# Local-attention scores as 64-row products per head, and value products on 64-key halves with 32-row edges

## The chip, the cores and the metric

The kernel runs on one NeuronCore of a Trainium2 chip. The time is the device time of one execution in microseconds (us). The runs of the kernel before have a median of 3595.3 us (three runs, 3594.93 to 3595.39).

## The reference, cut to what matters

The input is 16 sequences of 256 tokens with 128 features, all float32. First comes one causal attention layer with 16 heads of 8 features. Its output, layer-normalised, enters a stack of six layers, and each layer does, for every sequence:

```python
qkv = x @ Wqkv                                   # 128 -> 3 * 1024
q, k, v = 16 heads of 64
q, k = l2norm, times a scale, rotary turn
# local attention: windows of 32 queries, each sees its own 32 keys and the 32 before them
sim  = einsum('bhwie,bhwje->bhwij', bq, bk2) * 8     # 32 queries x 64 keys
attn = softmax(where(mask, -big, sim))               # j from i to i + 32 only
out  = einsum('bhwij,bhwje->bhwie', attn, bv2)       # 64 keys x 64 features
x = x + out @ Wo
# half of the features shifted by one token, layer norm, gated feed-forward
x = x + (a * gelu(gate)) @ W2 + b2
```

The change concerns the two einsum lines of the local attention.

## The kernel before, in words

The unit of work in the stack is one sequence in one layer, so there are 96 units, in order of layers. A sequence is two tiles of 128 tokens (t = 0 and 1). The first layer (causal attention) comes before and is not touched.

**The pipeline.** Each engine has its own queue, written out by hand in a function `step`, and works strictly in that order; semaphores tie the queues together. Step n works on three units at once: the "head" of unit n (projections of q, k, v and their norms), the "mid" of unit n-1 (turning q and k, scores, softmax, band) and the "ffn" of unit n-2 (values of tile 1, output projection, feed-forward). 94 of the 98 steps hold all three parts.

**PSUM.** `PJ` is the two banks of the projections, `TR[0]` and `TR[1]` are one bank each for transposes and the hidden layer, `EXO` and `EXY` half a bank each for the outputs. `SC` is two banks, `SC[:, 0]` and `SC[:, 1]`. They hold the scores of 8 heads each, and, in turn with them, the products with the values.

**Scores** (`scores(n, t, g)`, line 1389). g is a half of the heads and a bank. Before it, ScalarE writes the additive mask into the bank (`put_mask`, line 665) and the product is added to it. Two heads share 128 rows of `qT` (64 rows each). The keys are stored in `kbd` as a block-diagonal pair: head 0's keys in rows 0 to 63 with zeros under them, head 1's in rows 64 to 127 with zeros above. One product of 128 rows, 32 queries and 2 x 64 columns so gives two heads of one window. A block has 16 products, 4 windows in 4 column groups of the array, each writing 32 partitions. `k_evac` (lines 647 and 648) copies the turned keys into `kbd` in two instructions of 64 partitions each.

**Softmax.** VectorE takes the row maximum (`row_max`, line 901) and subtracts it (`less_max`, line 906), for each half g; ScalarE takes the exponential of a whole tile (`exps`, line 603); VectorE sums (913, 916), GpSimd normalises (462), and VectorE turns the tile in 32x32 blocks into `PTr[t]` (`turn`, line 923).

**Band and values.** SyncE's queue copies `PTr[t]` with DMAs into `BD`, which for each of four windows is a zero matrix of 128 keys with a band of 64 keys filled (`band`, lines 309 and 311, 7 DMAs a tile). For tile 1 the queries of the first window also need the last 32 keys of tile 0: `BB` (4 DMAs) holds their weights and `Vx` (4 DMAs, `edge_values`) the values. `values(n, t, g)` (lines 1344 and 1349) multiplies 128 keys by 4 windows of 32 queries for each of the 8 heads of half g, and for tile 1 adds the edge with two more products. ScalarE copies the result to `oT` (`o_evac`, line 672), and `output` (line 1356) multiplies by Wo.

**Order on TensorE in a full step** (m = n-1, f = n-2): turn_x(n), turn_k(m,0,0), output(f,0), turn_k(m,0,1), project_q(n,0), turn_q(m,0,0), values(f,1,0), turn_q(m,0,1), values(f,1,1), scores(m,0,0), output(f,1), scores(m,0,1), turn_q(m,1,0), turn_q(m,1,1), turn_k(m,1,0), project_v(n,0), scores(m,1,0), turn_k(m,1,1), project_k(n,0), scores(m,1,1), turn_xn(f), project_v(n,1), hidden(f,0), hidden(f,1), project_q(n,1), values(m,0,0), hidden(f,2), values(m,0,1), project_k(n,1), feed_out(f).

**Order on ScalarE**, the part around the change: q_evac(m,0,0), o_evac(f,1,0), put_mask(m,0,0), o_evac(f,1,1), q_evac(m,0,1), put_mask(m,0,1), squares, put_mask(m,1,0), q_evac(m,1,0), q_evac(m,1,1), exps(m,0), k_evac(m,1,0), put_mask(m,1,1), v_evac(n,0), rsqrt_guess(f) (lines 512 and 514), k_evac(m,1,1), keep_raw(n,0,k), xn_evac(f), squares, exps(m,1), v_evac(n,1), the gelus, ...

**Order on VectorE**, the same part: row_max and less_max(m,0,0), residual1(f) (line 1001, waits for output(f,1)), row_max and less_max(m,0,1), sum_q, soft_sum(m,0), x2_moments(f) (waits for the DMAs of the shift that start from residual1), row_max(m,1,0), ln_roots(f) (1026 to 1030), turn(m,0), layer_norm(f) (line 1038, whose result turn_xn(f) waits for), less_max(m,1,0), row_max and less_max(m,1,1), sum_k, soft_sum(m,1), cosines, gated(f,0), turn(m,1), ...

The trace counts passes: every float32 product runs as two passes with a weight load each, so a block of 16 products appears as x32. A transpose is one pass.

Of the kernel before, what the change touches and what calls it, by code (L numbers as in the profile page):

```python
# [10 lines left out]
ACT = mybir.ActivationFunctionType  # L11
# [38 lines left out]
def build(nc, x_in, wq_t, wk_t, wv_t, wo_t, wqkv, q_scale, k_scale, wo2, ln_g, ln_b, w1, b1, w2, b2,  # L50
          c_ident, c_winmask, c_causal, c_headmask, c_rot, out):
    with ExitStack() as ctx:
# [3 lines left out]
        def sem(name):  # L56
# [85 lines left out]
        names = ("d_x d_x2 d_wa d_wap d_rot d_c d_wq d_wk d_wv d_qks d_wo d_ln d_ff d_out i_const i_zero i_pad i_dve i_pool i_sp i_guess i_bits d_id d_wav d_hm "  # L142
# [5 lines left out]
                 "s_tab s_ct s_nq s_nk d_bd0 d_bd1 d_vx")  # L148
        S = {n: sem(n) for n in names.split()}
        (d_x, d_x2, d_wa, d_wap, d_rot, d_c, d_wq, d_wk, d_wv, d_qks, d_wo, d_ln, d_ff, d_out, i_const, i_zero, i_pad, i_dve, i_pool, i_sp, i_guess, i_bits, d_id, d_wav, d_hm,  # L150
# [5 lines left out]
         s_tab, s_ct, s_nq, s_nk, d_bd0, d_bd1, d_vx) = [S[n] for n in names.split()]  # L156
# [13 lines left out]
        N_BAND = (2 * NWIN - 1, 2 * NWIN - 1 + 4)  # L170
        N_VX = 4
# [68 lines left out]

        def turn_of_k(n, t):
            return 4 * n + (4 if t else 1)
# [13 lines left out]
        def _(sp):  # L256
# [46 lines left out]
            def band(n, t):  # L303

                need_apart(sp, i_sp, s_T, 2 * n + t + 1)
                need_apart(sp, i_sp, s_o, 4 * n + 2 * t - 2)
                for w in range(NWIN):
                    rows = slice(32 * w, 32 * w + 32)
                    sp.dma_start(BD[rows, t, w, :, :], PTr[t][rows, 1, :, :]).then_inc(d_bd[t], 16)
                    if w:  # L310
                        sp.dma_start(BD[32 * w - 32:32 * w, t, w, :, :], PTr[t][rows, 0, :, :]).then_inc(d_bd[t], 16)
                if t:
                    edge = PTr[t][0:WIN, 0, :, :].rearrange("p (g c k) i -> p g c (k i)", g=2, c=4)
                    for c in range(4):
                        sp.dma_start(BB[32 * c:32 * c + 32, :, c, :, :].rearrange("p g k i -> p g (k i)"),
                                     edge[:, :, c, :]).then_inc(d_bd[t], 16)

            def edge_values(n, par):

                need_apart(sp, i_sp, s_ve, 2 * n + 1)  # L320
                need_apart(sp, i_sp, s_o, 4 * n - 4)
                last = V[par][P - WIN:P, 0, :].rearrange("p (g c n) -> p g c n", g=2, c=4)
                for c in range(4):
                    sp.dma_start(Vx[32 * c:32 * c + 32, par, :, :], last[:, :, c, :]).then_inc(d_vx, 16)
# [10 lines left out]
            def step(n, u, par, head, mid, ffn, layer, more=False):  # L335
# [28 lines left out]
        def _(pool):  # L364
# [9 lines left out]
            pool.memset(BB[:, :, :, :, :], 0.0).then_inc(i_zero, 1)  # L374
            pool.wait_ge(d_hm, 16)
            pool.wait_ge(i_zero, 5)
# [13 lines left out]
            def a_step(n, par, head, mid, tail):  # L390
                if head:
                    spread_k(n, par)
                    if isinstance(n, int) and n == 0:
                        pool.memset(kbd[:, :, :, :], 0.0).then_inc(i_zero, 1)
# [106 lines left out]
        def _(act):  # L501
# [88 lines left out]
            act.wait_ge(i_zero, 7)  # L590
# [43 lines left out]
            def v_evac(n, t, par):  # L634
                T = 2 * n + t
                need(act, s_pv, T + 1)
                need(act, s_o, 4 * n - 4)
                act.activation(V[par][:, t, :], PJ[:, :], ACT.Copy).then_inc(s_ve, 1)  # L638

            def k_evac(n, t, g):  # L640
# [3 lines left out]
                need(act, s_sc, 4 * n - 1 + g)  # L644
                c = slice(4 * g, 4 * g + 4)
                at = slice(WIN + P * t, WIN + P * t + P)
                act.activation(kbd[0:DH, c, 0, at], tr[0:DH], ACT.Copy)
                act.activation(kbd[DH:P, c, 1, at], tr[DH:P], ACT.Copy).then_inc(s_te[g], 1)  # L648

            def q_evac(n, t, g):  # L650
                T = 2 * n + t
                need(act, s_tr[g], turn_of_q(n, t))
                need(act, s_sc, 2 * T - 1 + g)
# [14 lines left out]
            def o_evac(n, t, g):  # L668
                need(act, s_o, 4 * n + 2 * t + g + 1)
# [879 lines left out]
```

## Time and profile before

| | |
|---|---|
| median of the runs | 3595.3 us |
| span of the profiled execution | 3598.4 us |
| TensorE busy | 3482.8 us, 97% |
| VectorE busy | 3160.0 us, 88% |
| ScalarE busy | 3061.0 us, 85% |
| GpSimd busy | 2352.0 us, 65% |
| score passes (L1389) | 12288, busy 415.6 us |
| value passes (L1344, L1349) | 6144 and 768, busy 421.5 and 74.7 us |

The profile holds one execution; its span from the first to the last instruction is all that the page gives of its time, and it is 3.1 us over the median of the runs. Busy time counts overlapping instructions once. A TensorE row in a timeline ends with the modelled end of its last pass, about 0.1 to 0.2 us after the engine could take the next one; where one row starts before the one above has ended, the difference of the starts is what the first really took.

### The profile page before, as it was taken

How to read it: one execution, taken by the hardware profiler on the slowest of the kernel's cores; microseconds unless marked ns; L12 is line 12 of the kernel's file. 1: busy time of each engine (PE TensorE's matmuls, PEld its weight loads, DVE VectorE, ACT ScalarE, POOL GpSimd, SP SyncE). 2: the span in 40 equal slices, each digit the busy share in tenths (PEclk: the TensorE clock that was granted, in tenths of full speed). 3: DMA queues.
4: the chain of work that ended last, by engine and by line, in shares of the span. 5: the costliest groups of instructions: out<-in, count | busy, mean ns of one | idle time of the engine just before them, and what ended most of it. 6: DMA issues, size and time to landing. Idle time of an engine off the chain costs nothing.

```text
span 3598.4 us, 95666 instructions
## 1 busy us (share of the span) xinstructions
PE 3482.8 (97%) x33868; PEld 2390.4 (66%) x33868; DVE 3160.0 (88%) x5848; ACT 3061.0 (85%) x5121; POOL 2352.0 (65%) x1607
## 2 busy tenths in 40 slices
PE   8999899999999999999999999999999999999998
PEld 6777466666666666666666666666666666666666
DVE  6998889888988988888888898888889888888986
ACT  5766688888888888888888888888888888888886
POOL 2001677777777777777777677777777777777774
PEclk9999999999999999999999999999999999999999
DMA  2000011112211112211112111112111112211112
GB/s 63 0 0 0 21 34 39 38 33 54 52 34 34 39 36 52 50 40 33 34 40 53 46 39 38 32 36 58 47 33 39 38 33 55 52 33 34 39 37 54
DMA packets 182965, 136.67 MB, mean 38 GB/s; under 512 B 97612, under 2 KB 135632, under 8 KB 182800
## 3 DMA queue, kind: packets, MB, share of 16 engines
q1 hardware_dynamic: 180019, 125.00, 14.8%
q10 hardware_dynamic: 2781, 9.51, 0.9%
q8 instruction: 98, 1.61, 0.2%
q14 instruction: 67, 0.55, 0.1%
HBM read 19.04 MB, written 2.10 MB: 6 GB/s over the span
## 4 chain that ended last, share of the span: by engine, by line
PE 62%; ACT 19%; issue 10%; DVE 5%; SPq 1%; POOL 1%; DMA 1%; ACTq 0%; DVEq 0%; POOLq 0%
PE ps L1302 12%; PE ps L1389 10%; PE ps L1356 10%; PE ps L1344 7%; PE ps L1379 4%; PE ps L1370 4%; PE ps L1160 3%; ACT L750 3%; ACT area L603 2%; DVE area L987 2%; ACT G L609 2%; ACT L609 2%; ACT area L618 2%; ACT area L625 2%; PE ps L1295 2%
## 5 line engine op out<-in xcount | busy, mean ns | idle before, releaser
L1302 PE MATMUL ps<-Wqkv,xsT 128*128 128x512 f32 x2304 | 1112.5, 605 | 8.7 <-ACT area L638 3.8
L449 POOL TENSOR_TENSOR area<-area,tab 128x512 f32<-128x512 f32 x768 | 970.0, 1273 | 146.7 <-ACT area L618 146.1
L1302 PEld LDWEIGHTS ps<-Wqkv,xsT 128*128 128x128 f32 x2304 | 391.2, 189 | 351.4 <-issue 295.0
L462 POOL TENSOR_TENSOR area<-area,lsum 128x1024 f32<-128x1024 f32 x192 | 365.5, 1904 | 383.2 <-DVE lsum L916 383.2
L456 POOL TENSOR_TENSOR AQb<-AQb,area 128x1024 f32<-128x1024 f32 x192 | 455.2, 2371 | 15.1
L456 POOL TENSOR_TENSOR area<-area 128x1024 f32<-128x1024 f32 x192 | 455.0, 2370 | 9.0 <-DVE area L976 1.5
L618 ACT ACTIVATE area<-ps 128x1024 f32<-128x1024 f32 x384 | 393.6, 1025 | 66.2 <-PE ps L1302 55.1
L1389 PEld LDWEIGHTS ps<-kbd,area 128*32 128x32 f32 x12288 | 313.2, 109 | 196.1 <-issue 113.4
L1344 PE MATMUL ps<-BD,area 128*64 128x128 f32 x6144 | 421.5, 279 | 17.7 <-issue 11.3
L1344 PEld LDWEIGHTS ps<-BD,area 128*64 128x64 f32 x6144 | 329.4, 137 | 158.8 <-issue 100.2
L1389 PE MATMUL ps<-kbd,area 128*32 128x128 f32 x12288 | 415.6, 276 | 17.0 <-ACT kbd L648 5.7
L625 ACT ACTIVATE area<-area 128x1024 f32<-128x1024 f32 x384 | 405.1, 1055 | 3.2
L1356 PE MATMUL ps<-Wo,area 128*128 128x128 f32 x3072 | 385.2, 279 | 1.2 <-ACT area L672 0.7
L1356 PEld LDWEIGHTS ps<-Wo,area 128*128 128x128 f32 x3072 | 357.6, 192 | 20.7 <-issue 19.6
L654 ACT ACTIVATE area<-ps 128x512 f32<-128x512 f32 x384 | 217.9, 593 | 132.6 <-PE ps L1379 132.6
L901 DVE TENSOR_REDUCE mx<-ps 128x8 f32<-128x512 f32 x384 | 263.2, 686 | 49.7 <-PE ps L1389 49.7
L923 DVE STREAM_TRANSPOSE area<-area 128x1024 f32<-128x1024 f32 x192 | 239.2, 1246 | 61.7 <-POOL area L462 61.2
L1295 PE MATMUL ps<-xnT,W 128*128 128x256 f32 (+1 forms) x1152 | 288.3, 386 | 1.8 <-ACT xnT L684 1.5
L672 ACT ACTIVATE area<-ps 128x512 f32<-128x512 f32 x384 | 227.0, 591 | 71.0 <-PE ps L1349 66.8
L906 DVE TENSOR_TENSOR area<-ps,mx 128x512 f32<-128x512 f32 x384 | 264.8, 690 | 9.9
L1295 PEld LDWEIGHTS ps<-xnT,W 128*128 128x128 f32 (+1 forms) x1152 | 197.8, 178 | 91.3 <-issue 63.6
L941 DVE TENSOR_REDUCE ss<-area 128x16 f32<-128x1024 f32 x192 | 233.6, 1216 | 22.4 <-ACT area L625 21.2
(136 smaller groups left out, 6630.6 us busy)
## 6 DMA issues: line engine op xcount, KB each, us to landing
BD<-area SPq DMA_DIRECT2D x1344, 64.0 KB, 2.0
Vx<-area SPq DMA_DIRECT2D x384, 32.0 KB, 1.9
Wqkv<-ffn_Wqkv ACTq DMA_DIRECT2D x18, 512.0 KB, 4.0
BB<-area SPq DMA_DIRECT2D x384, 16.0 KB, 1.8
x2s<-x2s SPq DMA_DIRECT2D x96, 56.0 KB, 2.0
Wo<-ffn_Wo SPq DMA_DIRECT2D x6, 512.0 KB, 4.3
W<-ffn_W SPq DMA_DIRECT2D x6, 341.0 KB
x2s<-x2s SPq DMA_DIRECT2D x96, 0.2 KB, 1.7
```

What stands on the lines that cost most here:

```text
L449: pool.tensor_tensor(b4[:, :, here], q4[:, :, there], s4[:, :, here], ALU.mult).then_inc((s_bq, s_bk)[j], 1)
L456: pool.tensor_tensor(AQ[t][:, col], AQ[t][:, col], BQ[:, col], ALU.add).then_inc(s_rot, 1)
L462: pool.tensor_tensor(p3, p3, lsum[:, 1, :].unsqueeze(2).broadcast_to([P, HEADS, 2 * WIN]), ALU.mult).then_inc(s_pn, 1)
L618: act.activation(QH[:, j * INNER:(j + 1) * INNER], PJ[:, :], ACT.Copy).then_inc((s_hq, s_hk)[j], 1)
L625: act.activation(SQ[:, col], QH[:, col], ACT.Square).then_inc((s_sqq, s_sqk)[j], 1)
L901: dve.tensor_reduce(mx[:, 8 * g:8 * g + 8], s3[:, g, :, :], AX.X, ALU.max).then_inc(s_mx, 1)
L906: dve.tensor_tensor(Pr[:, t, 512 * g:512 * g + 512].rearrange("p (h k) -> p h k", k=2 * WIN), s3[:, g, :, :], mx[:, 8 * g:8 * g + 8].unsqu ...
L1295: last = mm(TR[c % 2][0:m, half * SEQ:(half + 1) * SEQ], W1[:, half * FF + f0:half * FF + f0 + m], xnT[:, :], start=True, stop=True)
L1302: last = mm(PJ[:, b * 512:(b + 1) * 512], xsT[:, par, t * P:(t + 1) * P], Wqkv[:, w0:w0 + 512], start=True, stop=True)
L1344: last = mm(slot[DH * k:DH * k + DH, c * P:(c + 1) * P], V[par][:, t, h * DH:(h + 1) * DH], BD[:, t, :, h, :], start=(c == 0), stop=False, ...
L1356: last = mm(EXO[:, t * P:(t + 1) * P], oT[:, t, c, :], Wo[:, c, :], start=(c == 0), stop=(c == PAIRS - 1))
L1389: last = mm(SC[32 * w:32 * w + 32, g, (c % 4) * P:(c % 4 + 1) * P], qT[:, c, 32 * w:32 * w + 32], kbd[:, c, :, k0:k0 + 2 * WIN], start=Fal ...
```

## The change

Scores become one product per head and window: the 64 rows of the head's q and of its keys, in the 64-row half of the array where they lie. The keys lose their zeros (`kT`), and are copied in one instruction. The even head of a pair writes bank 0 and the odd head bank 1, so one call now fills both banks, and there is one `scores` call a tile instead of two. Where the heads lie in a score tile changes with it (`place`).

Values: the band of a tile is now two halves of 64 keys with two windows of queries each (`BD`), and the windows that reach 32 keys into the half (or the tile) before get these as 32-row products (`BE`). The first half of the keys writes bank 0, the second bank 1; one `values` call a tile replaces two. `BB`, `Vx` and their DMAs go, and tile 1 has 8 band DMAs instead of 11.

The waits of these two calls on TensorE go through `need_apart`, which waits and then raises a semaphore that nobody waits for. Nothing is changed in the order of the other engines' queues: `row_max`, `less_max`, `put_mask`, `o_evac` stay at their places and work bank by bank.

```diff
-        kbd = sb("kbd", [P, PAIRS, 2, WIN + SEQ])
-        BD = sb("BD", [P, TILES, NWIN, HEADS, WIN])
-        BB = sb("BB", [P, 2, 4, 2, WIN])
-        Vx = sb("Vx", [P, 2, 2, P])
+        kT = sb("kT", [P, PAIRS, WIN + SEQ])
+        BD = sb("BD", [P, TILES, 2, HEADS, WIN])
+        BE = sb("BE", [P, TILES, HEADS, WIN])
...
+        def place(h):
+            return (h % 2) * PAIRS + h // 2
...
             def band(n, t):
                 need_apart(sp, i_sp, s_T, 2 * n + t + 1)
-                need_apart(sp, i_sp, s_o, 4 * n + 2 * t - 2)
+                need_apart(sp, i_sp, s_o, 2 * n + t - 1)
+                rows = [slice(32 * w, 32 * w + 32) for w in range(NWIN)]
                 for w in range(NWIN):
...
+                    sp.dma_start(BD[rows[w], t, w % 2, :, :], PTr[t][rows[w], 1, :, :]).then_inc(d_bd[t], 16)
+                    if w % 2:
+                        sp.dma_start(BD[rows[w - 1], t, 1, :, :], PTr[t][rows[w], 0, :, :]).then_inc(d_bd[t], 16)
+                    elif w or t:
+                        sp.dma_start(BE[rows[w - 1], t, :, :], PTr[t][rows[w], 0, :, :]).then_inc(d_bd[t], 16)
...
                 if mid:
                     band(n - 1, 0)
-                    edge_values(n - 1, 1 - par)
                     band(n - 1, 1)
...
             def k_evac(n, t, g):
...
-                need(act, s_sc, 4 * n - 1 + g)
-                c = slice(4 * g, 4 * g + 4)
+                need(act, s_sc, 2 * n)
                 at = slice(WIN + P * t, WIN + P * t + P)
-                act.activation(kbd[0:DH, c, 0, at], tr[0:DH], ACT.Copy)
-                act.activation(kbd[DH:P, c, 1, at], tr[DH:P], ACT.Copy).then_inc(s_te[g], 1)
+                act.activation(kT[:, 4 * g:4 * g + 4, at], tr, ACT.Copy).then_inc(s_te[g], 1)
...
             def o_evac(n, t, g):
-                need(act, s_o, 4 * n + 2 * t + g + 1)
+                need(act, s_o, 2 * n + t + 1)
...
             def row_max(n, t, g):
                 T = 2 * n + t
-                need(dve, s_sc, 2 * T + g + 1)
+                need(dve, s_sc, T + 1)
...
+            def values(n, t, par):
+
+                need_apart(pe, i_pe, s_ve, 2 * n + t + 1)
+                need_apart(pe, i_pe, d_bd[t], 16 * N_BAND[t] * (n + 1))
+                if t:
+                    need_apart(pe, i_pe, s_oe, 4 * n + 2)
+                else:
+                    need_apart(pe, i_pe, s_sub, 4 * n + 4)
+                for c in range(PAIRS):
+                    for r in range(2):
+                        keys = slice(2 * WIN * r, 2 * WIN * (r + 1))
+                        for k in range(2):
+                            h = 2 * c + k
+                            mm(SC[DH * k:DH * k + DH, r, 2 * WIN * c:2 * WIN * (c + 1)], V[par][keys, t, h * DH:(h + 1) * DH],
+                               BD[keys, t, :, place(h), :], start=(c == 0), stop=False, skip_group_check=True)
+                for c in range(PAIRS):
+                    for k in range(2):
+                        h = 2 * c + k
+                        last = mm(SC[DH * k:DH * k + DH, 1, 2 * WIN * c:2 * WIN * c + WIN], V[par][WIN:2 * WIN, t, h * DH:(h + 1) * DH],
+                                  BE[WIN:2 * WIN, t, place(h), :], start=False, stop=True, skip_group_check=True)
                     if t:
+                        for k in range(2):
+                            h = 2 * c + k
+                            last = mm(SC[DH * k:DH * k + DH, 0, 2 * WIN * c:2 * WIN * c + WIN], V[par][P - WIN:P, 0, h * DH:(h + 1) * DH],
+                                      BE[P - WIN:P, t, place(h), :], start=False, stop=True, skip_group_check=True)
                 last.then_inc(s_o, 1)
...
+            def scores(n, t):
+
+                ready = turn_of_k(n, 1) if t else turn_of_q(n, 0)
+                need_apart(pe, i_pe, s_mk, 4 * n + 2 * t + 2)
+                need_apart(pe, i_pe, s_te[0], ready)
+                need_apart(pe, i_pe, s_te[1], ready)
+                for c in range(PAIRS):
                     for w in range(NWIN):
                         k0 = P * t + WIN * w
+                        for k in range(2):
+                            half = slice(DH * k, DH * k + DH)
+                            last = mm(SC[32 * w:32 * w + 32, k, 2 * WIN * c:2 * WIN * (c + 1)],
+                                      qT[half, c, 32 * w:32 * w + 32], kT[half, c, k0:k0 + 2 * WIN],
+                                      start=False, stop=True, skip_group_check=True)
                 last.then_inc(s_sc, 1)
...
                 if ffn:
-                    values(n - 2, 1, 0, par)
+                    values(n - 2, 1, par)
                 if mid:
                     turn_q(n - 1, 0, 1)
                 if ffn:
-                    values(n - 2, 1, 1, par)
-                if mid:
-                    scores(n - 1, 0, 0)
-                if ffn:
                     output(n - 2, 1)
                 if mid:
-                    scores(n - 1, 0, 1)
+                    scores(n - 1, 0)
                     turn_q(n - 1, 1, 0)
...
                 if mid:
-                    scores(n - 1, 1, 0)
                     turn_k(n - 1, 1, 1)
...
                 if mid:
-                    scores(n - 1, 1, 1)
+                    scores(n - 1, 1)
...
-                if mid:
-                    values(n - 1, 0, 0, 1 - par)
                 if ffn:
                     hidden(n - 2, 2)
                 if mid:
-                    values(n - 1, 0, 1, 1 - par)
+                    values(n - 1, 0, 1 - par)
```

## Rows read from the trace of the kernel before

**Rows 1.** The page: span, and busy time of each engine.
```profile
span 3598.4 us, 95666 instructions
PE 3482.8 (97%) x33868; PEld 2390.4 (66%) x33868; DVE 3160.0 (88%) x5848; ACT 3061.0 (85%) x5121; POOL 2352.0 (65%) x1607
```

**Rows 2.** Timeline of TensorE: start, duration, line, shapes, count [idle before, releaser].
```profile
1688.89 1.09 PE L1344 MATMUL ps<-BD,area 128*64 128x128 f32 x16
...
1690.13 1.08 PE L1389 MATMUL ps<-kbd,area 128*32 128x128 f32 x32
1691.14 2.05 PE L1356 MATMUL ps<-Wo,area 128*128 128x128 f32 x16
1693.13 1.08 PE L1389 MATMUL ps<-kbd,area 128*32 128x128 f32 x32
1694.14 1.09 PE L1379 MATMUL ps<-ident,AQb 128*128 128x128 f32 x8
1695.58 0.65 PE L1370 MATMUL ps<-ident,AQb 128*128 128x128 f32 x4 [0.35 <-ACT area L654]
1696.07 1.88 PE L1302 MATMUL ps<-Wqkv,xsT 128*128 128x512 f32 x4
1698.08 1.08 PE L1389 MATMUL ps<-kbd,area 128*32 128x128 f32 x32
```

**Rows 3.** Timeline of TensorE one unit later, the same place.
```profile
1728.62 0.66 PE L1370 MATMUL ps<-ident,AQb 128*128 128x128 f32 x4 [0.33 <-ACT area L654]
```

**Rows 4.** Timeline of TensorE in two windows of 0.05 and 0.03 us.
```profile
1690.13 0.32 PE L1389 MATMUL ps<-kbd,area 128*32 128x128 f32 x4
...
200.83 0.38 PE L1149 MATMUL ps<-area,AqT 32*128 32x128 f32 x2
```

**Rows 5.** Timeline of ScalarE around the scores.
```profile
1690.25 0.60 ACT L672 ACTIVATE area<-ps 128x512 f32<-128x512 f32 x1 [0.60 <-PE ps L1349]
...
1692.83 0.60 ACT L665 ACTIVATE ps<-wmask_f 128x512 f32<-128x512 f32 x1
1694.93 1.09 ACT L654 ACTIVATE area<-ps 128x512 f32<-128x512 f32 x2 [1.49 <-PE ps L1379]
...
1696.85 0.58 ACT L647 ACTIVATE kbd<-ps 64x512 f32<-64x512 f32 x1
...
1698.54 1.03 ACT L638 ACTIVATE area<-ps 128x1024 f32<-128x1024 f32 x1
```

**Rows 6.** Timeline of VectorE around the scores.
```profile
1692.11 0.69 DVE L906 TENSOR_TENSOR area<-ps,mx 128x512 f32<-128x512 f32 x1
1693.36 0.42 DVE L1001 TENSOR_TENSOR x2s<-ps,xres 128x256 f32<-128x256 f32 x1 [0.56 <-PE ps L1356]
1694.27 0.69 DVE L901 TENSOR_REDUCE mx<-ps 128x8 f32<-128x512 f32 x1 [0.49 <-PE ps L1389]
...
1699.52 0.69 DVE L901 TENSOR_REDUCE mx<-ps 128x8 f32<-128x512 f32 x1
```

**Rows 7.** Timeline of all engines: layer_norm and the transpose behind it.
```profile
1701.86 0.57 DVE L1038 SCALAR_TENSOR_TENSOR xn<-x2s,mv,ps 128x128 f32<-128x128 f32 x2
...
1702.55 0.44 PE L1285 MATMUL ps<-ident,xn 128*128 128x128 f32 x2
```

**Rows 8.** Timeline of TensorE: rows that follow a long idle time.
```profile
397.34 2.65 PE L1389 MATMUL ps<-kbd,area 128*32 128x128 f32 x64 [1.85 <-ACT ps L665]
...
1942.45 1.09 PE L1344 MATMUL ps<-BD,area 128*64 128x128 f32 x16 [1.56 <-issue]
...
3566.46 1.97 PE L1344 MATMUL ps<-BD,area 128*64 128x128 f32 x16 [2.34 <-issue]
```

**Rows 9.** Windows after them: busy time by engine, granted clock, DMA share, GB/s.
```profile
398.70:402.00 3.30, 3.18 (x36) 2.40 (x26) 2.85 (x5) 0.73 (x2) 1.67 (x2) 0.50 0.03 7
...
1942.40:1946.00 3.60, 3.55 (x37) 2.57 (x38) 2.92 (x4) 2.02 (x3) 3.60 (x5) 1.00 0.52 174
...
3566.40:3569.40 3.00, 2.94 (x19) 2.32 (x20) 1.61 (x2) 0.00 (x0) 1.05 (x1) 0.50 0.21 44
```

More of the change, by code:

```diff
@@ L155, in build @@
          s_o, s_oe, s_ve, s_wo, s_r1, d_sh, s_lnc, s_lnr, s_lnn, s_ln, s_xn, s_xne, s_h, s_gl, s_g, s_y, s_xc,
-         s_tab, s_ct, s_nq, s_nk, d_bd0, d_bd1, d_vx) = [S[n] for n in names.split()]
+         s_tab, s_ct, s_nq, s_nk, d_bd0, d_bd1) = [S[n] for n in names.split()]
         PJ = ps[:, 0:2, :].rearrange("p a b -> p (a b)")
@@ L169, in build @@
         N_FF = 8
-        N_BAND = (2 * NWIN - 1, 2 * NWIN - 1 + 4)
-        N_VX = 4
+        N_BAND = (2 * NWIN - 1, 2 * NWIN)
         d_bd = (d_bd0, d_bd1)
@@ L589, in _ @@
             attention_steps(act, a_step)
-            act.wait_ge(i_zero, 7)
+            act.wait_ge(i_zero, 6)
             def x_evac(n, par):
@@ L668, in o_evac @@
             def o_evac(n, t, g):
-                need(act, s_o, 4 * n + 2 * t + g + 1)
+                need(act, s_o, 2 * n + t + 1)
                 if t == 0 and g == 0:
                     need(act, s_wo, n)
-                act.activation(oT[:, t, 4 * g:4 * g + 4, :], SC[:, g, :].rearrange("p (c n) -> p c n", c=4),
+                half = slice(2 * WIN * g, 2 * WIN * (g + 1))
+                act.activation(oT[:, t, :, half], SC[:, g, :].rearrange("p (c n) -> p c n", c=PAIRS),
                                ACT.Copy).then_inc(s_oe, 1)
@@ L1326, in project_v @@
                 projected(n, t, par, 2, s_pv)
-            def values(n, t, g, par):
-                T = 2 * n + t
-                if g == 0:
-                    need(pe, s_ve, T + 1)
-                    if t:
-                        need(pe, d_vx, 16 * N_VX * (n + 1))
-                    need(pe, d_bd[t], 16 * N_BAND[t] * (n + 1))
-                if t:
-                    need(pe, s_oe, 4 * n + g + 1)
-                else:
-                    need(pe, s_sub, 4 * n + 3 + g)
-                slot = SC[:, g, :]
-                for c in range(4):
-                    for k in range(2):
-                        h = 2 * (4 * g + c) + k
-                        last = mm(slot[DH * k:DH * k + DH, c * P:(c + 1) * P], V[par][:, t, h * DH:(h + 1) * DH],
-                                  BD[:, t, :, h, :], start=(c == 0), stop=False, skip_group_check=True)
-                if t:
-                    for k in range(2):
-                        half = slice(DH * k, DH * k + DH)
-                        last = mm(slot[half, :].rearrange("p (c n) -> p c n", c=4)[:, :, 0:WIN], Vx[:, par, g, half],
-                                  BB[:, g, :, k, :], start=False, stop=True, skip_group_check=True)
@@ L1380, in turn_q @@
                 last.then_inc(s_tr[g], 1)
-            def scores(n, t, g):
-                need(pe, s_mk, 4 * n + 2 * t + g + 1)
-                need(pe, s_te[g], turn_of_k(n, 1) if t else turn_of_q(n, 0))
-                for c in range(4 * g, 4 * g + 4):
+            def scores(n, t):
[4 more added lines that the diff above has]
+                for c in range(PAIRS):
                     for w in range(NWIN):
                         k0 = P * t + WIN * w
-                        last = mm(SC[32 * w:32 * w + 32, g, (c % 4) * P:(c % 4 + 1) * P],
-                                  qT[:, c, 32 * w:32 * w + 32], kbd[:, c, :, k0:k0 + 2 * WIN],
-                                  start=False, stop=True, skip_group_check=True)
+                        for k in range(2):
[3 more added lines that the diff above has]
+                                      start=False, stop=True, skip_group_check=True)
                 last.then_inc(s_sc, 1)
```

30 lines of the change are left out of this document (7 added, 23 removed).

## The prediction, as written before the changed kernel was run

> **What bounds the kernel now.** I read the page first. The reader is to see that TensorE is busy 97% of the span, VectorE 88% and ScalarE 85% [rows 1]. So TensorE's queue sets the pace, but two engines stand close behind it, and their queues were laid out around TensorE's order. Next the timeline of TensorE over one unit. The same transposes, behind the same short wait, start at 1695.58 and at 1728.62: a unit takes 33.04 us [rows 2, 3]. In it TensorE waits 0.35 us for ScalarE ahead of those transposes, and 0.29 ahead of the third score block, which starts at 1698.08 where the projection of 1696.07 (1.88 less an overlap of 0.16, so 1.72) ends at 1697.79 [rows 2]. With about 0.3 for small ones (my estimate) the waits are 0.95 a unit. There are 94 units in the full pattern, so 1 us a unit is 94 us, 2.6% of the time.
>
> **What TensorE gains: scores.** A block of 32 passes takes 1.01 us (1690.13 to 1691.14, and 1693.13 to 1694.14), and there are four a unit: 4.04 us [rows 2]. The four column groups work side by side: in a window of 0.05 us four passes have started [rows 4]. So 32 passes are eight rounds of 128 columns, about 0.11 each, and 0.14 remains for getting in from the whole array. The new block has 128 passes of 64 columns, eight tiles to a round, so 16 rounds. If the two 64-row halves run side by side, a round is 0.055 and the block 0.88 + 0.14, say 1.03. For the halves the trace has no row; the nearest is the causal layer, where two passes in different 32-row groups start within 0.03 us and write different banks [rows 4], as the two heads do here. I take 1.03 (bounds 0.9, and 1.9 if the halves take turns). Two blocks are 2.06: a gain of 1.98.
>
> **Values.** A 16-pass block takes 1.09 less 0.07 of overlap, 1.02, and with the edge of tile 1 1.24 (1688.89 to 1690.13) [rows 2]: 2 x 1.02 + 2 x 1.24 = 4.52 a unit. The new call has 64 passes of 64 columns on four tiles (16 rounds of 0.055), then an edge part of 32 passes on two tiles or 64 on four (16 rounds). The edge has only 32 columns but loads 64 weight columns, so I give it 0.055 a round too. With 0.14 for getting in and 0.14 for the change from 64 to 32 rows: 0.88 + 0.88 + 0.28 = 2.04, twice 4.08, a gain of 0.44. Bounds for one call: 1.5 if the edge goes at the speed of its columns, 2.9 and 3.9 (tiles 0 and 1) if row groups take turns.
>
> **Fewer changes of shape.** Output takes 1.99 (1691.14 to 1693.13) where 16 passes at 0.11 are 1.76 [rows 2]: of the 0.23, some 0.16 is the way back to the whole array. Eight blocks become four, which gives 0.65. TensorE gains 1.98 + 0.44 + 0.65 = 3.1 us a unit, 29.0 of work instead of 32.1.
>
> **What it loses: the two banks no longer take turns.** Today, while one half of the heads is with VectorE or ScalarE, TensorE works on the other. Now a call needs both banks and frees both, while the queues of the other engines stay as they are. I walk these queues with the row durations. A block's result reaches the next engine 0.13 us after it (1694.14 to 1694.27) [rows 2, 6]; between engines I add 0.08.
>
> (a) output(f,1) needs both o_evac. Behind the values ScalarE does o_evac, put_mask, o_evac (0.60, 0.60, 0.60 [rows 5], in sequence with overlap 1.75), so it can start 0.13 + 1.75 + 0.08 = 1.96 after the values. In that time TensorE has turn_q, 0.59 behind a block. Wait 1.4. Today the first o_evac and the mask run under the second block.
>
> (b) turn_k(m,1,0) needs q_evac(m,1,0), which on ScalarE stands behind put_mask(m,1,0), which needs the first less_max. From the end of scores: 0.13 + row_max 0.71 (0.69 and a gap of 0.02) + less_max 0.69 + 0.08 + mask 0.60 + q_evac 0.55 + 0.08 = 2.84 [rows 5, 6]. TensorE has two calls of turn_q, 1.04. Wait 1.8, in place of 0.35. Today output(f,1) and the second block cover this chain.
>
> (c) project_k needs v_evac, behind exps. VectorE after scores: 0.13 + 0.71 + 0.69, residual1 0.42 (rounded up to 0.45), row_max 0.71, less_max 0.65 (with overlap), 0.08: 3.4. ScalarE then does exps 0.97 (1.03 for this size, less overlap, as in v_evac's row), k_evac 0.55 (one instruction at a 128x512 copy's time, in place of two of 0.58), put_mask 0.58, v_evac 0.95 [rows 5]: 6.5. TensorE is there at 2.84 + turn_k 0.50 + project_v 1.74 + turn_k 0.44 = 5.5. Wait 1.0, and 0.2 more ahead of scores(m,1), for the last k_evac.
>
> (d) turn_xn needs layer_norm. On VectorE this stands behind row_max(m,1,0), the three small ln_roots and turn(m,0). Today row_max starts at 1699.52, under the transposes and project_k, and the xn rows from 1701.86 to 1702.43 are just in time for the transpose at 1702.55 [rows 6, 7]. In the new order scores(m,1) is one block directly ahead of turn_xn, and row_max can't start before its end. Start of row_max to end of xn is 2.91 without a gap, so the wait is 0.13 + 2.91 = 3.0. This is the largest, and it hangs on no unknown of the array.
>
> (e) Behind turn_xn ScalarE's and VectorE's queues are late as well (they have xn_evac, squares, sum_k, soft_sum(m,1), cosines and gated(f,0) to do before hidden(f,2) can start), while TensorE comes through its four projections and hidden blocks at its old speed. I allow 0.9 for what it waits at project_q(n,1) and hidden(f,2), an estimate with bounds 0 and 2.
>
> Sum of waits: 1.4 + 1.8 + 1.0 + 0.2 + 3.0 + 0.9 = 8.3, less today's 0.95. A unit grows by 8.3 - 0.95 - 3.1 = 4.2 us, to 37.3. Over 94 units that is 395 us.
>
> **What costs nothing.** ScalarE's four k_evac save 2.3 us a unit, but the walk has them in it. Of the DMAs 7 of 22 in a unit go; the values of tile 0 wait for their 7 either way, and the layer's turn(m,0) to values(m,0) grows longer, so they stay hidden. The added semaphore increments are off the chain as long as their semaphores are early; they stop TensorE's sequencer from running ahead, up to 0.1 at a block that was late (between 0 and 0.4 a unit; I take 0). The causal layer is untouched.
>
> **The clock.** Three idle stretches of TensorE, the first and last of them 1.85 and 2.34 us, were each followed by a stretch at half clock (0.50, 1.2 GHz); one of 1.56 was not, and the clock stayed at 1.00 (2.4 GHz) [rows 8, 9]. Values passes took 1.97 for 16 there, against 1.09 [rows 2, 8]. Wait (d) is 3.0 and comes in every unit, so I expect half clock behind it in most: about 3.3 us in which 1.7 of work takes 3.4. Of the extra 1.7, the 0.9 of (e) is absorbed, and the rest delays ScalarE's gelus: 1.0 a unit, in 0.8 of the units 75 us.
>
> **The sum.** The span is 3598.4 and the median of runs 3595.3; the 3 us between them don't matter to a growth, which I add to the median: 3595 + 395 + 75 = 4065 us.
>
> **A page that speaks against the change.** In a window of 0.05 us four passes on different column groups start, and 32 take 1.01 us, 31.6 ns each [rows 2, 4]. The Trainium skill, "TensorEngine Tiling (Array Packing)", section "Instruction Overhead", says that each matmul has some 60 cycles of overhead on this chip and that a dimension already small should not be tiled. If that held per pass and not per tile, 25 ns at 2.4 GHz (an estimate from that page), scores would take 3.2 and values 2.4 and 3.2, and the result would be near 4540; the rows speak for the shared reading.
>
> **Rivals.**
> 1. No half clock, or seldom: 3595 + 395 = 3990. For it: the waits of 1.56 and less left the clock alone. Chance 0.27.
> 2. The row halves take turns, or passes are bound by their number. With 1.9 for scores and 2.9 and 3.9 for values the calls add 2 x 0.87 + 0.86 + 1.86 = 4.5: 395 + 420 gives about 4410. At today's 31.6 ns for every pass they would be 4.04, 3.03 and 4.04, 9.0 more a unit: some 4840. Against it: rows 4. Chance 0.13.
> 3. Half clock behind (b) as well, 1.8 long and near the 1.85 that was enough once: another 1.2 a unit, 4180. Chance 0.10.
> 4. Faster. If the waits were covered as they are today, the unit would fall from 33.04 to the busy time of VectorE, 88.5% of it or 29.3, and about 1 of its waits: 30.3, in all 3340. It decides at (d): row_max(m,1,0) would have to come before TensorE wants turn_xn. Faster blocks alone don't do it: at the low bounds, 0.9 and 1.5, a unit still takes 37.3 - 0.3 - 1.1 = 35.9, so the sign turns only where (d) and one more wait are covered. Chance 0.04.
> The likeliest (0.46) is 4065.
>
> **How the numbers follow.** What can be told from no change is about 0.2%. Only rival 4 is faster, and a part of 0.02 I leave for waits that just balance the gain; slower has the rest, 0.94. The range goes from below rival 1 with a short edge part (a unit 1 us less: 3900) to above rival 3 (4260); left out are rival 2, rival 4 and the ends.
>
> **What would show it.** Score passes: x128 blocks of about 1.0 us, twice a unit. Ahead of turn_xn about 3 us of idle TensorE, released by VectorE's layer_norm; ahead of output(f,1) 1.4 by o_evac, of turn_k(m,1,0) 1.8 by q_evac, of project_k(n,0) 1.0 by v_evac. TensorE's share of busy time falls from 97% to about 80%. The clock: dips behind turn_xn, mean well under 1. The forecast is wrong if the wait at turn_xn is under 2 us, or if the score blocks take over 1.5 us.

## The result, and the profile after

Before 3595.4 us (median of five runs, 3594.9 to 3596.6), after 4342.9 us (five, 4341.4 to 4367.4): 1.209 times as long, 95% interval 1.207 to 1.212. The direction was forecast. The size was not: the growth is 748 us where 470 were forecast, and 4343 lies above the top of the range, 4260. The profiled execution is the slowest of the five, 4367.4 us, some 25 over the median. Of all runs of this document one, of the last kernel below, took 5050.6 us at a granted clock of 0.635 and is left out.

The page of the profile after, at the same places as [rows 1], with the queue of the transfers that bring instructions:

```profile
span 4365.6 us, 148729 instructions
PE 3597.4 (82%) x60748; PEld 2539.6 (58%) x60748; DVE 3172.5 (73%) x5848; ACT 2841.7 (65%) x4737; POOL 2341.1 (54%) x1606
q8 instruction: 521, 8.54, 0.8%
```

All engines fell to 54 to 82%: nothing is full, so TensorE waits. Its waits (engine, line waited for, us in total, times, longest):

```profile
PE ps L1272 <- DVE xn L1025: 280.5, 96, 3.3
PE ps L1359 <- ACT area L640: 152.2, 96, 1.7
PE ps L1345 <- ACT area L659: 122.2, 97, 1.3
PE ps L1289 <- ACT area L626: 72.6, 98, 3.9
PE ps L1382 <- issue: 50.0, 27, 2.4
PE ps L1266 <- issue: 33.7, 30, 1.7
```

The first four are the forecast ones, (d), (b), (a) and (c), about once in each of the 96 units. The last two were not forecast, and no other engine releases them; all waits named "issue" add to 100 us, before to 12.

To see the order of the work alone, take a unit in which the clock stayed up. The timeline of TensorE from one turn_x to the next, which is what [rows 2] show of before (start, duration, line, shapes, count, idle before):

```profile
2745.22 0.43 PE L1266 MATMUL ps<-ident,xst 128*128 128x128 f32 x2 [1.22 <-issue]
...
2750.40 1.16 PE L1328 MATMUL ps<-BD,area 64*64 64x64 f32 x64
...
2752.55 0.66 PE L1368 MATMUL ps<-ident,area 128*128 128x128 f32 x4
2754.49 2.05 PE L1345 MATMUL ps<-Wo,area 128*128 128x128 f32 x16 [1.28 <-ACT area L659]
2756.47 1.49 PE L1382 MATMUL ps<-kT,area 64*32 64x64 f32 x128
2757.88 1.09 PE L1368 MATMUL ps<-ident,AQb 128*128 128x128 f32 x8
2760.61 0.65 PE L1359 MATMUL ps<-ident,AQb 128*128 128x128 f32 x4 [1.63 <-ACT area L640]
...
2764.12 1.99 PE L1289 MATMUL ps<-Wqkv,xsT 128*128 128x512 f32 x4 [0.70 <-ACT area L626]
...
2770.55 0.44 PE L1272 MATMUL ps<-ident,xn 128*128 128x128 f32 x2 [3.03 <-DVE xn L1025]
...
2777.14 1.09 PE L1282 MATMUL ps<-xnT,W 128*85 128x256 f32 x4 [0.69 <-DVE H L916]
...
2783.47 0.38 PE L1266 MATMUL ps<-ident,xst 128*128 128x128 f32 x2
```

The unit takes 38.25 us (2745.22 to 2783.47), before 33.04. A score block takes 1.41 (2756.47 to 2757.88; forecast 1.03), the value call 2.15 (2750.40 to 2752.55; forecast 2.04). The five waits are 1.28, 1.63, 0.70, 3.03 and 0.69. An idle time in this view starts at the modelled end, some 0.1 after the engine was free; from start to start, as the forecast counts, they are about 1.35, 1.7, 0.9, 3.1 and 0.85, together 7.9 (forecast 8.3).

Few units are like this one: only six of the 93 periods between the turn_x of full units have no stretch at half clock, and the three of them that hold no wait named "issue" take 38.3 us on the mean. The mean of the 93 is 41.2. Windows of another unit show the rest (the columns as in [rows 9]: busy time of TensorE, weight loads, VectorE, ScalarE and GpSimd, then granted clock, DMA share, GB/s):

```profile
2008.00:2011.50 3.50, 2.16 (x88) 1.75 (x79) 1.20 (x2) 1.82 (x4) 1.30 (x1) 1.00 0.02 5
2011.80:2015.20 3.40, 3.33 (x16) 3.28 (x16) 1.20 (x2) 1.97 (x4) 0.00 (x0) 0.55 0.00 0
2015.30:2029.20 13.90, 8.70 (x281) 5.73 (x280) 9.13 (x21) 6.68 (x11) 8.18 (x6) 0.98 0.03 7
2029.80:2033.10 3.30, 3.30 (x5) 1.28 (x5) 2.74 (x8) 2.45 (x3) 0.77 (x1) 0.50 0.40 99
```

Two stretches at half clock (0.50, 1.2 GHz; 1.00 is 2.4) in one unit. The first begins at 2011.47, inside wait (a), and lasts into output(f,1); the second begins at 2028.54, inside wait (d), and covers the work behind turn_xn. The trace has 151 such stretches, 4.3 us long on the mean: 57 begin in output(f,1) or the wait ahead of it, 89 in the wait ahead of turn_xn, in turn_xn or in the projection behind it. The mean clock of this execution is 0.926, so 2 x 0.074 x 4365.6 = 646 us of it ran at half clock; before, 0.998 and about 14.

And the unforecast wait, inside a score block:

```profile
2065.22 1.21 PE L1382 MATMUL ps<-kT,area 64*32 64x64 f32 x101
2068.48 0.44 PE L1382 MATMUL ps<-kT,area 64*32 64x64 f32 x27 [2.05 <-issue]
```

101 passes of the block run, then TensorE stands for 2 us with its operands ready, then the other 27. The only DMA traffic between 2065.5 and 2068.5 is one packet of the instruction queue, on its way from 2066.10 to 2067.21. That queue brought 521 packets of 16 KB; before it were 98, and none of them fell between 1695.6 and 1728.6. The whole trace bears this one case out. Of TensorE's 58 "issue" waits over 0.8 us, 56 end between 1.0 and 1.75 us after the end of a packet of this queue, where a tenth of all moments lie. Of the 8 such waits before the change, none does.

So I split the 748 us into three parts, which the experiments below test: (38.3 - 33.04) x 94 = 494 for the order of the work with its real block times, 161 for the clock (from the fillings below), and the remaining 93, which I put down to instruction fetching.

### The profile page after: what moved, and what is told of

It reads as the page before. It is cut to its first block, busy times and chain, and to the rows that moved or that the text cites. A ratio compares the mean times of both kernels' runs of the same rounds, so it can differ in the third digit from the quotient of the medians.

```text
span 4365.6 us, 148729 instructions
## 1 busy us (share of the span) xinstructions
PE 3597.4 (82%) x60748; PEld 2539.6 (58%) x60748; DVE 3172.5 (73%) x5848; ACT 2841.7 (65%) x4737; POOL 2341.1 (54%) x1606
## 4 chain that ended last, share of the span: by engine, by line
PE 69%; DVE 11%; issue 10%; ACT 9%; DMA 0%; DVEq 0%; SPq 0%; ACTq 0%; POOL 0%; POOLq 0%
PE ps L1289 22%; PE ps L1345 10%; PE ps L1382 7%; PE ps L1282 6%; PE ps L1328 4%; PE ps L1333 4%; DVE mx L888 3%; ACT area L659 3%; PE ps L1392 2%; PE ps L1147 2%; PE ps L1359 2%; ACT area L626 2%; DVE area L893 2%; DVE area L910 2%; PE ps L1139 1%
## 5 line engine op out<-in xcount | busy, mean ns | idle before, releaser
L1289 PE MATMUL ps<-Wqkv,xsT 128*128 128x512 f32 x2304 | 1245.1, 668 | 76.2 <-ACT area L626 72.6
L1345 PE MATMUL ps<-Wo,area 128*128 128x128 f32 x3072 | 457.4, 311 | 122.9 <-ACT area L659 122.2
L1345 PEld LDWEIGHTS ps<-Wo,area 128*128 128x128 f32 x3072 | 423.6, 221 | 148.7 <-ACT area L659 145.2
L651 ACT ACTIVATE ps<-wmask_f 128x512 f32<-128x512 f32 x384 | 230.5, 600 | 385.2 <-DVE area L893 382.2
L1382 PEld LDWEIGHTS ps<-kT,area 64*32 64x32 f32 x24576 | 269.5, 110 | 148.5 <-issue 142.9
L1382 PE MATMUL ps<-kT,area 64*32 64x64 f32 x24576 | 305.2, 235 | 54.7 <-issue 50.0
L963 DVE TENSOR_TENSOR area<-area,ps 128x1024 f32<-128x1024 f32 x192 | 228.7, 1191 | 98.1 <-PE ps L1368 97.3
L659 ACT ACTIVATE area<-ps 128x512 f32<-128x512 f32 x384 | 225.0, 587 | 108.0 <-PE ps L1338 106.6
L1272 PE MATMUL ps<-ident,xn 128*128 128x128 f32 x192 | 58.2, 399 | 280.5 <-DVE xn L1025 280.5
L634 ACT ACTIVATE kT<-ps 128x512 f32<-128x512 f32 x384 | 225.6, 588 | 90.3 <-PE ps L1359 87.9
```

The lines of the kernel that those rows point to most:

```text
L651: act.activation(SC[:, g, :].rearrange("p (h k) -> p h k", k=2 * WIN), wmask_f[:, t, :].unsqueeze(1).broadcast_to([P, HEADS // 2, 2 * WIN] ...
L659: act.activation(oT[:, t, :, half], SC[:, g, :].rearrange("p (c n) -> p c n", c=PAIRS), ACT.Copy).then_inc(s_oe, 1)
L1289: last = mm(PJ[:, b * 512:(b + 1) * 512], xsT[:, par, t * P:(t + 1) * P], Wqkv[:, w0:w0 + 512], start=True, stop=True)
L1345: last = mm(EXO[:, t * P:(t + 1) * P], oT[:, t, c, :], Wo[:, c, :], start=(c == 0), stop=(c == PAIRS - 1))
L1382: last = mm(SC[32 * w:32 * w + 32, k, 2 * WIN * c:2 * WIN * (c + 1)], qT[half, c, 32 * w:32 * w + 32], kT[half, c, k0:k0 + 2 * WIN], start ...
```

## The experiments

The theory: the growth is the waits of the walk, the half clock that they bring, and fetches. Rivals: the passes themselves cost it (too many, or the row halves take turns); the clock costs no more than the 75 us of the forecast; the stalls named "issue" are something other than fetching. Each kernel is the changed one with the edit shown, unless said otherwise.

### layer_norm ahead of the late scores on VectorE

```diff
-                if mid:
-                    row_max(n - 1, 1, 0)
                 if ffn:
...
                     layer_norm(n - 2, mid)
                 if mid:
+                    row_max(n - 1, 1, 0)
                     less_max(n - 1, 1, 0)
```

> The changed kernel with one move in VectorE's queue: ln_roots, turn(m,0) and layer_norm stand ahead of row_max(m,1,0) instead of behind it, so they no longer wait for the single score block. Theory A (the waits from the two banks and the unchanged queues make most of the loss, and long waits bring half clock): the 3.0 us wait at turn_xn goes; walking the queues with the durations of the trace gives 36.0 us a unit against 38.3 without clock losses, 216 us less over 94 units, and about 94 more because the longest wait is one of the two that bring half clock: about 4035 us (3950 to 4150). Theory B (the number of passes on TensorE sets the time): within 1% of 4343.

Measured 4079.4 us, ratio to before 1.133 (1.132 to 1.135): 263 us less than the change, from one line's place in VectorE's queue. The expectation was 4035. The waits of TensorE:

```profile
PE ps L1358 <- ACT area L640: 154.3, 96, 1.7
PE ps L1288 <- ACT area L626: 143.5, 175, 2.9
PE ps L1344 <- ACT area L659: 121.3, 97, 1.3
PE ps L1381 <- issue: 47.7, 27, 2.4
```

The 280.5 at the transposes of xn are gone from the list, and a quarter of them come back at the projections, which now wait twice as much for v_evac (72.6 to 143.5). Some of the gain is clock, 0.968 here. What is left of half clock is at the other place: 57 of its 76 stretches begin at output(f,1) or the wait ahead of it, as many as in the change, though the wait at turn_xn is gone. So the stretch at (a) doesn't come from the one at (d).

### TensorE kept busy in the three long waits

bfloat16 products that nobody reads, 5 ahead of output(f,1), 7 ahead of turn_k(m,1,0), 13 ahead of turn_xn. The last place is shown; at the other two a wait for the bank that they write stands ahead of them.

```diff
+                if head and mid and ffn:
+                    fill(TR[0][:, 0:512], 13)
                 if ffn:
                     turn_xn(n - 2)
```

> The changed kernel with bf16 products that nobody reads, put where TensorE waits: 13 ahead of turn_xn, 5 ahead of output(f,1), 7 behind turn_q(m,1,1), each 512 columns, about 0.21 us. They cover the waits without shortening them. Theory A: TensorE is never long idle, the granted clock stays at 1.00, and the 6.3 us of half clock a unit go; by units of the changed kernel with no half clock (38.2 to 38.6) against the mean of 41.0, less the stalls for instructions that remain, about 2 us a unit: 4150 (4080 to 4230). If half clock costs nothing (hidden by the waits): 4343 or a little more.

Measured 4182.4 us, 1.163 (1.161 to 1.165), mean clock 0.996. The unit keeps its order and its pace:

```profile
2402.62 1.67 PE L1405 MATMUL ps<-causal,ident_h 128*128 128x512 bf16 x7
2404.42 0.66 PE L1359 MATMUL ps<-ident,AQb 128*128 128x128 f32 x4
...
2411.26 2.98 PE L1405 MATMUL ps<-causal,ident_h 128*128 128x512 bf16 x13
2414.65 1.88 PE L1289 MATMUL ps<-Wqkv,xsT 128*128 128x512 f32 x4
```

More work on TensorE, and 161 us less time: the waits cost not only themselves but the clock behind them. The projection behind turn_xn takes 1.88 us here and in the clean unit, and 3.62 in a unit with half clock. Most of the 161 is therefore what half clock cost. Not all of it need be: TensorE's waits named "issue" also fell, from 100 to 74 us, most of it in the score blocks (50.0 to 13.9), so the clock's share is 135 to 161.

The run also separates the third part. 89 of the 93 periods have no half clock at all. The 45 of them without an "issue" wait take 38.3 us, as in the change, and the 44 with one take 39.7. Over the 89 the mean is 39.0, so 0.7 x 94, some 70 us, belongs neither to the order of the work nor to the clock.

### Scores alone, and values alone

The first keeps the 128-key bands and values in two blocks, with the new score call; the second keeps the block-diagonal keys and four score blocks, with the new value calls. Of each edit only a part of TensorE's order is shown.

```diff
@@ scores alone
-                    values(n - 2, 1, par)
+                    values(n - 2, 1, 0, par)
                 if mid:
                     turn_q(n - 1, 0, 1)
                 if ffn:
+                    values(n - 2, 1, 1, par)
                     output(n - 2, 1)
...
@@ values alone
+                if mid:
+                    scores(n - 1, 0, 0)
                 if ffn:
                     output(n - 2, 1)
                 if mid:
-                    scores(n - 1, 0)
+                    scores(n - 1, 0, 1)
...
```

> Only the scores are changed (64-row products per head, one block a tile, one k_evac instruction); the products with the values are those of before, on 128 keys, in two halves. Theory A: the walk gives 37.5 us a unit against 32.9 for before: +430 us, plus half clock as in the changed kernel, 100 to 180: about 4170 (4050 to 4260). Theory C (instruction code that no longer fits and is fetched again costs about 0.9 us a unit): if this smaller body fits, instruction packets stay near 98 and no stalls of 1.7 to 2.4 us stand inside score blocks. Theory B, passes: 128 more a unit of the 280, so about 340 us: 3940.

> Only the products with the values are changed (64-key halves, 32-row edges, one call a tile); the scores are those of before. Theory A: values(f,1) frees both banks at once, so scores(m,0,0) waits about 0.9 us for its mask and hidden(f,2) 0.7; the walk gives 34.2 us a unit against 32.9, +123 us, no wait over 1 us, so no half clock: 3720 (3660 to 3800). Theory B, passes: 152 more a unit of the 280: +405 us, 4000. Theory C: if the code fits, no instruction packets above 98.

Scores alone: 4240.0 us, 1.178 (1.176 to 1.180), clock 0.951. Values alone: 3773.4, 1.049 (1.047 to 1.051), clock 0.997. So 645 and 178 us by themselves, and 748 together; the two don't simply add. The longest waits of TensorE, scores alone and then values alone:

```profile
PE ps L1286 <- DVE xn L1039: 280.9, 96, 3.3
PE ps L1371 <- ACT area L655: 158.6, 96, 1.7
PE ps L1303 <- ACT area L641: 77.0, 98, 3.9
PE ps L1357 <- ACT area L673: 67.8, 97, 0.9
PE ps L1394 <- issue: 54.6, 32, 2.2
```

```profile
PE ps L1380 <- ACT ps L653: 79.7, 96, 1.9
PE ps L1284 <- DVE H L918: 69.4, 96, 2.2
PE ps L1268 <- issue: 39.5, 30, 1.7
PE ps L1361 <- ACT area L642: 33.4, 96, 1.2
```

Waits (b), (c) and (d) come whole with the joined score call, as the walk has them. (a) falls to 0.7 a unit, for the first of two value calls gives ScalarE an early start; and of the 84 stretches of half clock only 5 are left at output(f,1), 65 stand at turn_xn, its wait and the projection behind it. Values alone wait 0.8 a unit at a place of their own: the first score block has to wait for the mask, which stands between the two o_evac. The shortest units of it take 34.1 us, 2.0 of that in such waits. Instruction packets are 405 and 427: either half of the change is enough to bring fetches into the loops. (I had thought that each might stay near 98.)

### The kernel before, with a loop body twice as long

```diff
-                with eng.Fori(0, SEQS // 2 - 2) as k:
-                    for odd in range(2):
-                        step(eng.snap(base + 2 * k + (2 + odd)), 2 * k + (2 + odd), odd, True, True, True, layer)
+                with eng.Fori(0, (SEQS // 2 - 2) // 2) as k:
+                    for odd in range(4):
+                        step(eng.snap(base + 4 * k + (2 + odd)), 4 * k + (2 + odd), odd % 2, True, True, True, layer)
```

Every engine does exactly the work of before; only four units stand in a loop body in place of two.

> The kernel before with a loop body of four units instead of two (three turns of the loop a layer instead of six); every engine does the same work in the same order. Theory C (a body that is too long for what the core keeps of it is fetched again in every turn): instruction packets rise from 98 to about 300, each of the 18 turns has about 1.3 us of idle TensorE at its first instruction as in the changed kernel, and since this kernel has no fast score blocks there are few other stalls: +20 to +45 us, 3615 to 3640. If fetching is free or doesn't happen: within 0.2% of 3595, packets 98.

Measured 3658.4 us, 1.018 (1.016 to 1.019): 62 us for nothing but the length of the code. Its instruction queue and all but one of TensorE's waits of the kind "issue", then those of the unchanged kernel at the value products (whose queue brought 98 packets):

```profile
q8 instruction: 277, 4.54, 0.5%
...
PE ps L1279 <- issue: 25.6, 12, 2.5
...
PE ps L1344 <- issue: 13.0, 10, 4.0
...
PE ps L1356 <- issue: 4.2, 3, 1.9
```

```profile
PE ps L1344 <- issue: 11.3, 11, 2.3
```

The fetches fall into the loops, and TensorE stands at turn_x (L1279), the first work of a body, in 12 of the 18 turns, about 2 us each time. The waits at L1344 were there before. The 15 new ones, at L1279 and L1356, all end 1.1 to 1.9 us after the end of an instruction packet. This is the picture of the changed kernel's L1266 and L1382, without any small pass.

The cost was above what I expected (20 to 45), and these waits are only half of it: all of TensorE's "issue" waits grow by 32 us. VectorE's grow from 0.7 to 21.9 us, and the time at half clock from 14 to 34 us; how much of the other 30 us each of them makes is not shown.

### A score block cut in four

scores(m,0) with three unread bfloat16 products between each 32 passes and the next; one run.

```diff
+                    if parts and c in (2, 4, 6):
+                        fill(PJ[:, 0:512], 3)
                     for w in range(NWIN):
```

> The changed kernel with scores(m,0) cut in four parts of 32 passes, with three bf16 products of 512 columns that nobody reads (0.65 us) between the parts; scores(m,1) stays whole. It asks why a block takes 1.41 us and not 1.03. Theory D (the first 32 passes, 64 instructions with their weight loads, lie ready, and what follows comes no faster than the instructions are fed): each part takes 0.14 to get in and 0.22, so about 0.36. Theory E (the eight tiles disturb each other, the same for all passes): each part takes 0.14 + 1.27 / 4, about 0.46. The whole time is not what counts; about 4350 to 4450.

Timeline of TensorE:

```profile
2039.83 0.46 PE L1386 MATMUL ps<-kT,area 64*32 64x64 f32 x32
2040.22 0.82 PE L1409 MATMUL ps<-causal,ident_h 128*128 128x512 bf16 x3
2040.97 0.45 PE L1386 MATMUL ps<-kT,area 64*32 64x64 f32 x32
```

A part takes 0.39 (2039.83 to 2040.22), nearer to theory D (0.36) than to E (0.46). Less the 0.14 of entry that the forecast uses, 32 passes take 0.25, four times that 1.0; the whole block needs 1.41 - 0.14 = 1.27. In the unbroken block at 2024.85 the first 32 passes start as in such a part, within 0.24 us and mostly 7 ns apart. Then comes a gap of 0.08, and the last 96 start over 1.03 us, 10.7 ns apart on the mean. Each part here has the fast beginning again. The passes use the same tiles in all parts, so the tiles alone don't set the slower rate. That it is the supply of instructions is the likely reading and not shown, since one run doesn't tell it from a fixed cost of entry. (The run as a whole took 4577.9 us where up to 4450 was expected; it pays for the fillings and says nothing of this.)

### The queues put in the order that the walk asks for

layer_norm early as above, residual1 ahead of row_max(m,0,0), both o_evac ahead of the mask, both q_evac ahead of the mask. Then the same with unread products ahead of project_k. ScalarE's part of the edit is shown.

```diff
                     o_evac(n - 2, 1, 0)
-                if mid:
-                    put_mask(n - 1, 0, 0)
-                if ffn:
                     o_evac(n - 2, 1, 1)
                 if mid:
+                    put_mask(n - 1, 0, 0)
                     q_evac(n - 1, 0, 1)
...
-                    put_mask(n - 1, 1, 0)
                     q_evac(n - 1, 1, 0)
                     q_evac(n - 1, 1, 1)
+                    put_mask(n - 1, 1, 0)
```

> The changed kernel with four moves in the other queues: on VectorE ln_roots, turn(m,0) and layer_norm ahead of row_max(m,1,0), and residual1(f) ahead of row_max(m,0,0); on ScalarE o_evac(f,1,1) ahead of put_mask(m,0,0), and both q_evac(m,1) ahead of put_mask(m,1,0). Theory A: the walk gives 34.8 us a unit (38.3 as it was, 32.9 for before), so 3597 + 178, plus about 100 for fetched instructions and 30 to 80 of half clock, because 2.0 us of wait are left at project_k: 3920 (3870 to 3990). It stays slower than the kernel before. Theory B (number of passes): 4343, as the passes are the same.

> The same as the run with four moves, and ahead of project_k 16 bf16 products of 256 columns that nobody reads, 1.7 us, where its 2.0 us of wait is. Theory A with half clock: the granted clock stays at 1.00 and the time falls by the 30 to 80 us that half clock takes there, to about 3870. Without an effect of the clock: the same as without the products, or up to 20 us more.

Measured 3939.7 us, 1.095 (1.093 to 1.096), and 3896.1, 1.085 (1.083 to 1.087). 403 of the 748 us are regained by order alone, with the clock that it gives back (0.988). The longest waits of the first:

```profile
PE ps L1286 <- ACT area L626: 230.4, 177, 2.9
PE ps L1342 <- ACT area L659: 59.3, 96, 1.2
PE ps L1379 <- issue: 54.7, 34, 2.4
PE ps L1263 <- issue: 44.3, 30, 1.9
PE ps L1279 <- DVE H L914: 41.1, 89, 2.9
PE ps L1365 <- issue: 26.4, 17, 2.4
PE ps L1356 <- ACT area L640: 26.2, 86, 0.3
```

(b) falls from 152 to 26 and (a) from 122 to 59, but the projections now wait 230 us for v_evac (72.6 in the change). The shortest units take 34.9, still 1.9 over the 33.04 of before. The waits named "issue" grow from 100 to 149 us, and 84 of the 87 over 0.8 us end 1.0 to 1.75 us after an instruction packet (of TensorE's other waits of that size 5 of 183 do). So of the 344 us that this kernel is slower than before, about 180 are order and work, about 140 are these stalls, and the rest is what half clock still costs. No version of the whole change comes near the kernel before.

The unread products took another 44 us off. Half clock fell from 94 to 66 us in the profiled executions, but the "issue" waits fell from 149 to 98 too, so this pair doesn't separate the two.

Whether the added semaphore increments of `need_apart` cost anything (0 to 0.4 us a unit by the forecast's bounds) is shown by no run here.

## Why the prediction was right and where it was wrong

**Bound and mechanism: right.** The forecast said that TensorE's faster work would be more than lost to waits, because one call now needs and frees both banks while the other queues stay as they were. The waits came where they were put: (a) 1.4, (b) 1.8 and (d) 3.0 were met within 0.1; (c) measured 0.9 against 1.0 + 0.2, (e) 0.85 against 0.9. That they are set by the order of the queues is shown by the two reordered kernels (263 and 403 us regained), and that the score call carries most of them by the two halves.

**Score block: mis-sized.** "I take 1.03" measured 1.41. The halves do run side by side: 128 passes in 1.41 us are 11 ns each, where before a pass took 31.6 [rows 2]. The forecast took it that passes can be supplied at any rate that the array takes. Within its bounds (0.9 to 1.9), yet 2 x 0.38 x 94 = 71 us. The value call, 2.15 for 2.04, adds 2 x 0.11 x 94 = 21. Together 92. The waits were 0.4 a unit less than forecast and TensorE's other work, by difference, 0.4 more, which cancels: the unit of 37.3 becomes 38.3, and 395 becomes 494. So the change saved TensorE not 3.1 us of work a unit but about 1.7 (32.1 less 30.4).

**The clock: mis-sized by half.** "1.0 a unit, in 0.8 of the units 75 us" measured 135 to 161. The forecast let half clock come only behind (d). A second stretch lies at output(f,1) or in wait (a) ahead of it in more than half of the units. Rival 3 had put one behind (b), with a further 1.2 a unit (113 us) and a chance of 0.10. The rule taken from [rows 8, 9], that 1.56 of idle time leaves the clock alone, was one sighting: here the clock fell in or behind idle times of 1.27, with a value call and eight transposes between them and the last projection. Whether the small tiles ahead of the wait or the other waits near it do that is open; that it isn't wait (d) is shown by the early layer_norm.

**What costs nothing: the step that failed outright.** The paragraph lists DMAs, semaphores and k_evac, and has no line on the code itself. The passes in a unit rise by (60748 - 33868) / 96 = 280, and the profile's instruction queue stood at 98 packets, with none inside the loop's units: a row that I could have read and did not. The cost is 93 us as the remainder of the sum, and some 70 from the units with the clock held up; the waits named "issue" add to 88 us more than before. That more code alone does this is shown on the kernel before (62 us). In the changed kernel itself the cause was not removed by an experiment, since any shorter body is another kernel; there it rests on the packets, behind which 56 of 58 stalls end at the same distance.

**The sum.** 395 + 75 + 0 was forecast, 494 + 161 + 93 came, where up to 26 of the 161 may belong to the 93. None of the three alone leaves the range: 4065 + 99 is 4164, with the clock 4250. It is the fetches on top that carry it past 4260.

**The rivals.** Rival 1 (no half clock, 3990) is refuted by the granted clock of 0.926. Rival 2 (row halves in turns, or 31.6 ns a pass, 4410 to 4840) is the trap of this case: its lower time is closer to 4343 than the forecast is, and yet its mechanism is wrong, for it needs blocks of 1.9. It is the same with the rule of the Trainium skill ("TensorEngine Tiling (Array Packing)", "Instruction Overhead") that was weighed: read per pass, 25 ns, it gave 4540 and a block of 3.2. The block measured 1.41, so the rule doesn't hold per pass when the passes lie on different tiles, as the four-in-0.05 us of [rows 4] had said. Rival 3 was the nearest in mechanism: half clock did come at a second place, though at (a) and not at (b). Rival 4 (faster than before if the waits were covered) did not come about. The early layer_norm covered (d) and the four moves most of (b) and half of (a) as well, but the unit stayed at 34.9, where rival 4 named 30.3, because v_evac was uncovered instead.

**What would show it.** Waits, busy share (forecast about 80%, measured 82%) and dips of the clock came as written; "x128 blocks of about 1.0 us" did not, and stayed under the 1.5 that would have made the forecast wrong.

## What to carry to other kernels

Before TensorE's blocks are made faster by joining them, ask which other engine's work ran under the first of the two; here 1.7 us of work saved a unit (3.1 by the forecast) brought 7 us of new waits. When the change multiplies the number of passes, read the packets of the instruction queue inside a loop's unit before and price the loop body's length as a cost of its own. And price a wait together with the clock that may fall in it or behind it.

## What was not expected of the hardware

- The length of a loop body has a price: the same work with four units in a body in place of two took the instruction packets from 98 to 277 and the time from 3597 to 3658 us, with TensorE idle about 2 us at the start of 12 of 18 bodies.
- A stall for instructions can be told in the trace: in the changed kernel 56 of 58 "issue" waits over 0.8 us end 1.0 to 1.75 us after the end of a packet of the instruction queue.
- A long run of small passes slows after its first 32: mostly 7 ns from start to start, then 10.7 on the mean, 128 in 1.27 us after entry where four separate runs of 32 would take 1.0.
- Half clock came in more than half of the units (57) in or behind a wait of about 1.27 us with a call of small tiles ahead of it, where a wait of 1.56 before had not been followed by it [rows 8, 9]. A projection then took 3.62 us in place of 1.88.
- 25 unread products a unit, laid in the waits, made the changed kernel 161 us faster.
